# Reordering TensorE's and ScalarE's steps in the second attention pass of a graph network, and pairing the small operations of its dense pass

## The chip, the cores and the metric

One Trainium2 chip; the kernel runs on one of its cores. The metric is the device time of one execution in microseconds (us), lower is better. TensorE does matmuls and transposes, VectorE and ScalarE element-wise work, GpSimd element-wise work and indirect transfers (gathers and scatters of rows), and SyncE (SP) only issues direct transfers. All five run their own queues in order and meet at semaphores.

## The reference

Four layers over a graph of N = 50,000 nodes with 256 features and E = 12,500 edges, each with residual and layer norm:

```python
x = _layernorm(x + gin(x, src, dst, edge_weight))      # sums over edges, two dense layers with batch norm
x = _layernorm(x + gat(x, edge_index, W, a))           # attention over edges, rows without an edge give 0
x = _layernorm(x + attention(x, edge_attr_8, Wq, Wk, Wv, Wo, src, dst))
x = _layernorm(x + self_loop_gat(x, edge_index, W, att_src, att_dst, bias))   # every node has a loop
# of the third:
attn = einsum('ehd,ehd->eh', k[src], q[dst]) + attn_bias
a = exp(attn - segment_max(attn, dst)[dst]);  a = a / segment_sum(a, dst)[dst]
out = segment_sum(v[src] * a[:, :, None], dst).reshape(n, F) @ Wo.T
```

A node that no edge reaches keeps what the layers make of its own row alone: three layer norms in a row, and in the last layer `elu(x3 @ W + bias)`. There are only 12,500 edges for 50,000 nodes, so most nodes are of this kind.

## The kernel before

The program is a chain of phases with a barrier between two of them. First the edges are sorted and the first layer's sums are made; `mlp` computes its dense layers, feature-major, into `Y2`. Then come the two passes that the change touches, with the edge pass of the second layer (`gat_edges`) and the scores of the third between them.

**The dense pass, `nodes` (L1121 to L1355).** It computes for every node what it would be without edges, and stores the rows after layers one and two (`X1`, `X2`) and the final one (`out`). The work is cut in 100 chunks of 500 nodes (one load and one store of each tensor), and each chunk in two tiles of 250 nodes (125 partitions, J = 2 rows each). Per tile: ScalarE `relu` (batch norm and relu of `Y2` into `z`); TensorE `turn_z`; VectorE `add` (u = z + x), `stats`, `aggregate`, `variances1` (three small operations that give the variances of three layer norms in a row); ScalarE `rsqrt1` (Ln and Exp); VectorE `means` (one operation on six elements); GpSimd `first_two` (x1 and x2, two operations each) and ScalarE `third` (x3); TensorE `turn_x3`, ScalarE `copy_x3`, TensorE `product`, ScalarE `exps`, VectorE `elus`, GpSimd `add` (v = elu + x3, one operation of 512 elements); VectorE `stats2`, `aggregate2`, `variances2`; ScalarE `rsqrt2`; VectorE `outs` (two operations).

Each engine's order is written out by hand as a list of (lag, step); `run_stages` goes through it once per iteration, and a step with lag k handles tile t - k in iteration t:

```python
PE    [(8, product), (6, turn_x3), (1, turn_z)]
ACT   [(12, rsqrt2), (9, exps), (7, copy_x3), (5, third), (3, rsqrt1), (0, relu)]
DVE   [(13, outs), (2, add), (11, stats2), (9, elus), (2, stats1), (11, aggregate2), (4, means), (2, aggregate1), (11, variances2), (2, variances1)]
POOL  [(10, add), (5, first_two)]
SP    [(8, store_out), (4, store), (0, load)]      # in chunks
```

**The second attention pass, `attention_sums` (L1928 to L2106).** It goes over 100 columns of 125 edges, sorted by destination, and a last one for sums that cross partitions: 101 iterations, tile 'at' below. VectorE makes weighted rows (`messages`), the running segment sum (`add`), `keep_lead`, `denominators`, `reciprocals` and `quotients`, which writes the normalised row sum `on` (L2092). TensorE turns `on` (`turn`, L1998), ScalarE copies it to `onT` (`copy`, L2040), TensorE multiplies by Wo (`product`, L2006), VectorE adds the node's row (`residual`, L2101: u) and takes its moments, ScalarE normalises it to x3 (`norm`), TensorE turns it (`turn_x3`, L2014, one PSUM buffer), ScalarE copies it (`copy_x3`, L2051), TensorE multiplies by the last layer's weights (`product_x3`, L2022 to L2024), and ScalarE takes that out of PSUM (`keep_xp`: L2056, and L2057 for `ends`). SP loads and stores rows, GpSimd scatters them. The orders:

```python
PE    [(0, carry_over), (7, product_x3), (5, turn_x3), (2, product), (1, turn)]
ACT   [(8, keep_xp), (5, copy_x3), (4, norm), (0, copy)]
DVE   [(0, messages), (3, residual), (0, add), (4, stats), (0, keep_lead), (0, denominators), (4, aggregate), (1, quotients), (0, reciprocals), (4, last)]
```

`product_x3` for tile t waits for `keep_xp` of tile t - 2 (two PSUM buffers), and `turn_x3` of tile t for `copy_x3` of tile t - 1.

## Time and profile before

| | |
|---|---|
| median of 3 runs | 4757.65 us (4750.59 to 4759.39) |
| the profiled execution | 4765.5 us, of which the span of its instructions is 4763.8 us |
| dense pass | 1766 to 2761 us |
| edge pass of layer two (not changed) | from about 2765 to 3420 us |
| second attention pass | 3774 to about 4206 us |

Times in the profile are counted from the start of the span. PE is TensorE's matmuls, PEld its weight loads, DVE VectorE, ACT ScalarE, POOL GpSimd. A line of the timeline merges equal instructions of one engine that follow each other; its brackets give the engine's idle time before and who ended it. The last instruction of the engine before may end a little after the next starts, since they are pipelined.

### The profile page before, as it was taken

What the parts mean: (1) busy time and instruction counts of PE and PEld (TensorE: products, weight loads), DVE (VectorE), ACT (ScalarE), POOL (GpSimd) and SP (SyncE); (2) the same over time, 40 slices, a digit from 0 to 9 for tenths busy, and PEclk for the clock granted to TensorE, in tenths of its full rate; (3) what the DMA queues carried; (4) which work ended last, traced back from release to release, by engine and by line L of the source; (5) the groups of instructions that cost most, each with busy time, mean ns of one, the idle gap of its engine ahead of it and who ended that gap; (6) DMA issues with size and microseconds to landing.
All of it is one profiled execution on the core that took longest, in us unless ns stands there. A gap on an engine that the chain in (4) does not pass through costs nothing. (4 is left out here: it accounts for less than half of the span.)

```text
span 4763.8 us, 90855 instructions
## 1 busy us (share of the span) xinstructions
PE 3204.6 (67%) x16514; PEld 2413.6 (51%) x16514; DVE 3460.4 (73%) x12339; ACT 2663.8 (56%) x6336; POOL 3034.6 (64%) x2926
## 2 busy tenths in 40 slices
PE   4999934447999988777777767777699577720000
PEld 2799812226888865555555545555588444410000
DVE  7788733335555559999999988888755666611998
ACT  0688712224666558878887758878644255510444
POOL 0466668883443337777777768888778355565888
PEclk9999955558999989999999977777699799965555
DMA  1788723333444448888888733333355266642343
GB/s 41 193 237 237 207 71 80 79 79 116 159 162 163 158 159 268 261 263 260 261 261 262 245 93 99 98 98 99 99 128 128 77 180 178 179 111 70 110 110 93
DMA packets 450180, 734.76 MB, mean 154 GB/s; under 512 B 171319, under 2 KB 284845, under 8 KB 450028
## 3 DMA queue, kind: packets, MB, share of 16 engines
q1 hardware_dynamic: 276204, 571.18, 39.8%
q0 software_dynamic: 173824, 162.17, 14.1%
q14 instruction: 131, 1.07, 0.1%
q8 instruction: 21, 0.34, 0.0%
HBM read 351.68 MB, written 389.16 MB: 156 GB/s over the span
## 5 line engine op out<-in xcount | busy, mean ns | idle before, releaser
L1209 PE MATMUL nodes_xp<-w_self,nodes_x3T 128*125 128x256 f32 x1600 | 448.4, 403 | 232.3 <-DVE nodes_elu L1315 232.3
L1081 POOL TENSOR_TENSOR mlp_r_parts<-mlp_r,mlp_r_parts 128x500 fp32r<-128x500 f32 x200 | 253.5, 1267 | 405.0 <-ACT mlp_r_parts L1067 395.7
L1345 POOL TENSOR_SCALAR nodes_x<-nodes_u,nodes_r,nodes_nm 125x256 f32<-125x256 f32 x800 | 448.3, 574 | 79.1 <-DVE nodes_nm L1308 79.1
L1209 PEld LDWEIGHTS nodes_xp<-w_self,nodes_x3T 128*125 128x125 f32 x1600 | 268.4, 187 | 312.3 <-issue 196.1
L1353 POOL TENSOR_TENSOR nodes_v<-nodes_elu,nodes_x 125x512 f32<-125x512 f32 x200 | 253.7, 1269 | 221.9 <-DVE nodes_elu L1315 220.8
L775 PE MATMUL gram<-gin_both,gin_am 125*128 125x257 f32 x404 | 206.1, 665 | 267.7 <-DVE gin_both L758 255.4
L1106 DVE BATCH_NORM_STATS2 mlp_stats<-mlp_y 128x500 f32 (+1 forms) x200 | 136.2, 681 | 256.9 <-ACT mlp_y L1057 256.9
L178 POOL DMA_INDIRECT by_src<-rank_recs,rank_place x100 | 119.7, 1197 | 289.9 <-DVE rank_recs L504 289.3
L775 PEld LDWEIGHTS gram<-gin_both,gin_am 125*128 125x128 f32 x404 | 118.1, 322 | 355.7 <-issue 324.2
L1020 PE MATMUL mlp_y<-mlp_hT,mlp_w 128*128 128x500 f32 x1200 | 297.0, 396 | 1.9 <-DVE mlp_hT L1100 1.2
L1020 PE MATMUL mlp_y<-mlp_r_parts,mlp_w 128*128 128x500 f32 x1200 | 287.3, 388 | 0.8 <-ACT mlp_y L1057 0.8
L564 PE MATMUL gram<-rank_xc 125*128 125x257 f32 (+1 forms) x1600 | 279.1, 328 | 0.0
L564 PEld LDWEIGHTS gram<-rank_xc 125*128 125x128 f32 x1600 | 249.2, 191 | 22.4
L728 DVE SCALAR_TENSOR_TENSOR gin_acc<-gin_acc,same,gin_msg 125x256 f32<-125x256 f32 x100 | 48.4, 484 | 287.4 <-ACT gin_msg L700 207.0
L1065 ACT ACTIVATE mlp_r<-mlp_y,affine 128x500 f32<-128x500 f32 x200 | 154.0, 770 | 182.7 <-PE mlp_y L1020 182.7
L178 POOL DMA_INDIRECT out<-att_fin,write x101 | 124.8, 1236 | 200.5 <-DMA att_fin<-G 193.8
L1020 PEld LDWEIGHTS mlp_y<-mlp_r_parts,mlp_w 128*128 128x128 f32 x1200 | 225.2, 188 | 47.4 <-POOL mlp_r_parts L1081 1.1
L1222 ACT ACTIVATE nodes_z<-nodes_y,affine 128x250 f32<-128x250 f32 x400 | 216.2, 588 | 50.7 <-ACT nodes_r L785 39.1
L1020 PEld LDWEIGHTS mlp_y<-mlp_hT,mlp_w 128*128 128x128 f32 x1200 | 218.0, 188 | 41.6 <-DVE mlp_hT L1100 1.4
L1816 PE MATMUL self_cps<-self_acc,carry 125*125 125x260 f32 x2 | 1.2, 716 | 352.4 <-DVE self_acc L1801 352.4
L700 ACT ACTIVATE gin_msg<-gin_xd,srec 125x256 f32<-125x256 f32 x100 | 50.7, 507 | 308.0 <-DMA gin_xd<-x,other 308.0
L1241 ACT ACTIVATE nodes_x<-nodes_u,nodes_nm,nodes_r 125x256 f32<-125x256 f32 x400 | 219.1, 601 | 0.0
(397 smaller groups left out, 11588.9 us busy)
## 6 DMA issues: line engine op xcount, KB each, us to landing
X<-nodes_x SPq DMA_DIRECT2D x200, 448.0 KB
Y<-mlp_y SPq DMA_DIRECT2D x100, 500.0 KB
nodes_y<-Y SPq DMA_DIRECT2D x100, 500.0 KB
rank_xin<-x SPq DMA_DIRECT2D x100, 448.0 KB
XP<-rank_xc SPq DMA_DIRECT2D x100, 448.0 KB
mlp_h<-XP SPq DMA_DIRECT2D x100, 448.0 KB
nodes_x<-x SPq DMA_DIRECT2D x100, 448.0 KB
out<-nodes_out SPq DMA_DIRECT2D x100, 448.0 KB
```

Of the source, the lines that this page charges most:

```text
L178: self.pool.indirect_dma_start(table, bass.IndirectOffsetOnAxis(index, 0), rows, None, bounds_check=self.bound, oob_is_err=False).then_inc ...
L564: mm = pe.matmul(gram[:, m, 128 * m:F + 1], xc[:, s, j, 128 * m:128 * m + 128], xc[:, s, j, 128 * m:F + 1], start=False, stop=True, skip_g ...
L775: mm = pe.matmul(gram[:, m, 0:F + 1], am[:, s, 128 * m:128 * m + 128], both[:, s, 0:F + 1], start=False, stop=True, skip_group_check=True)
L1020: mm = pe.matmul(out[:, m, 0:CH], w[:, a, k, 128 * m:128 * m + 128], rows[:, s, b, k, :], start=((k, a, b) == terms[0]), stop=((k, a, b) = ...
L1065: act.activation(r[:, s, m, :], y1[:, m, 0:CH], ACT.Relu, bias=aff[:, 1, m:m + 1], scale=aff[:, 0, m:m + 1]).then_inc(s_r, 1)
L1081: pool.tensor_tensor(rp[:, s, 1, m, :], r[:, s, m, :], rp[:, s, 0, m, :], ALU.subtract).then_inc(s_rp, 1)
L1106: dve.bn_stats(stats[:, m, at.col, :].rearrange("p o n -> p (o n)"), y[:, s, m, :]).then_inc(s_st, 1)
L1209: pe.matmul(xp[:, b, j, :], x3T[:, s, k, P * j:P * j + P], w_self[:, k, 0:F], start=(k == 0), stop=False)
L1222: act.activation(z[:, s, m, :], y[:, c, m, HC * h:HC * h + HC], ACT.Relu, bias=aff[:, 3, m:m + 1], scale=aff[:, 2, m:m + 1]).then_inc(s_z, 1)
L1241: act.activation(x3[:, at.slot(LONG), j, :], u[:, s, j, :], ACT.Identity, bias=nm[:, s, 2, j:j + 1], scale=r[:, s, 2, j:j + 1]).then_inc(s ...
L1345: pool.tensor_scalar(dst[:, s, j, :], u[:, s, j, :], r[:, s, k, j:j + 1], nm[:, s, k, j:j + 1], ALU.mult, ALU.add).then_inc(done, 1)
L1353: pool.tensor_tensor(v[:, s, :, :], el[:, s, :, :], x3[:, at.slot(LONG), :, :], ALU.add).then_inc(s_v, 1)
```

## The change

In `attention_sums` two lists change, TensorE's and ScalarE's; nothing of VectorE's, SP's or GpSimd's. TensorE's turn of `on` goes from last to first in an iteration, and `turn_x3` and `product_x3` get one lag more; on ScalarE, `copy` goes from last to first, and `keep_xp` from first to third, behind `copy_x3`.

In `nodes`, the small operations are done once for two tiles (in the iterations in which the step's tile is odd, `pairs_only`): `variances1`, `variances2`, `rsqrt1`, `rsqrt2` on twice as many elements, and `means` as three operations instead of one. `u` and `mv` get eight buffers instead of four. The chunks' load buffers `y` and `x` go from two to four, SP's loop from two to four chunks per turn, and its stores from lags 4 and 8 to 7 and 11. Every step after `means` gets one lag more, on all engines.

```diff
-    y, z = ph.sb("y", [128, 2, KH, CH]), ph.sb("z", [128, RING, KH, HC])
-    x, u = ph.sb("x", [P, RING, J, F]), ph.sb("u", [P, RING, J, F])
+    AHEAD = 4
+    y, z = ph.sb("y", [128, AHEAD, KH, CH]), ph.sb("z", [128, RING, KH, HC])
+    x, u = ph.sb("x", [P, 2 * AHEAD, J, F]), ph.sb("u", [P, LONG, J, F])
...
+    def both(at):
+        return slice(at.slot(RING) - 1, at.slot(RING) + 1)
+
+    def pairs_only(step):
+        return lambda at: step(at) if at.slot(PAIR) == 1 else None
...
-                wait(sp, s_z, at.count(4, 4 - 8))
+                c = at.slot(AHEAD)
+                wait(sp, s_z, at.count(4, 4 - 4 * AHEAD))
...
-                wait(sp, s_u, at.count(2, 2 - 4))
+                wait(sp, s_u, at.count(2, 2 - 2 * AHEAD))
...
-            run_stages(sp, [(8, store_out), (4, store), (0, load)], NCH, NCH, unroll=2)
+            run_stages(sp, [(11, store_out), (7, store), (0, load)], NCH, NCH, unroll=AHEAD)
...
-            run_stages(pe, [(8, product), (6, turn_x3), (1, turn_z)], tiles, tiles, LONG, LONG)
+            run_stages(pe, [(9, product), (7, turn_x3), (1, turn_z)], tiles, tiles, LONG, LONG)
...
+            @pairs_only
             def rsqrt1(at):
-                s = at.slot(RING)
-                act.wait_ge(s_q, at.count(3, 3))
+                p = both(at)
+                act.wait_ge(s_q, at.uses(PAIR, 3, 3))
...
-                rsqrt(act, ch, r[:, s, :, :], lnq[:, s, :, :], q[:, s, :, :])
+                rsqrt(act, ch, r[:, p, :, :], lnq[:, p, :, :], q[:, p, :, :])
...
-            run_stages(act, [(12, rsqrt2), (9, exps), (7, copy_x3), (5, third), (3, rsqrt1), (0, relu)], tiles, tiles, LONG, LONG)
+            run_stages(act, [(13, rsqrt2), (10, exps), (8, copy_x3), (6, third), (3, rsqrt1), (0, relu)], tiles, tiles, LONG, LONG)
...
+            @pairs_only
             def variances1(at):
...
-                    dve.tensor_scalar(q[:, s, k, :], mv[:, s, :, 1], m, a, ALU.mult, ALU.add).then_inc(s_q, 1)
+                    dve.tensor_scalar(q[:, p, k, :], mv[:, both_long(at), :, 1], m, a, ALU.mult, ALU.add).then_inc(s_q, 1)
...
+            @pairs_only
             def means(at):
...
-                dve.scalar_tensor_tensor(out=nm[:, s, :, :], in0=r[:, s, :, :], scalar=-1.0,
-                                         in1=mv[:, s, :, 0].unsqueeze(1).broadcast_to([P, 3, J]), op0=ALU.mult, op1=ALU.mult).then_inc(s_nm, 1)
+                for k in range(3):
+                    dve.scalar_tensor_tensor(out=nm[:, p, k, :], in0=r[:, p, k, :], scalar=-1.0,
+                                             in1=mv[:, both_long(at), :, 0], op0=ALU.mult, op1=ALU.mult).then_inc(s_nm, 1)
...
-                dve.tensor_scalar(q2[:, s, :], mv2[:, s, :, 1], EPS, None, ALU.add).then_inc(s_q2, 1)
+                dve.tensor_scalar(q2[:, p, :], mv2[:, p, :, 1], EPS, None, ALU.add).then_inc(s_q2, 1)
...
-            run_stages(dve, [(13, outs), (2, add), (11, stats2), (9, elus), (2, stats1), (11, aggregate2), (4, means), (2, aggregate1),
-                             (11, variances2), (2, variances1)], tiles, tiles, LONG, LONG)
+            run_stages(dve, [(14, outs), (2, add), (12, stats2), (10, elus), (2, stats1), (12, aggregate2), (4, means), (2, aggregate1),
+                             (12, variances2), (2, variances1)], tiles, tiles, LONG, LONG)
...
-            run_stages(pool, [(10, add), (5, first_two)], tiles, tiles, LONG, LONG)
+            run_stages(pool, [(11, add), (6, first_two)], tiles, tiles, LONG, LONG)
...
-            run_stages(pe, [(0, carry_over), (7, product_x3), (5, turn_x3), (2, product), (1, turn)], T + 1, unroll=LONG, behind=LONG)
+            run_stages(pe, [(0, carry_over), (1, turn), (8, product_x3), (6, turn_x3), (2, product)], T + 1, unroll=LONG, behind=LONG)
...
-            run_stages(act, [(8, keep_xp), (5, copy_x3), (4, norm), (0, copy)], T + 1, unroll=LONG, behind=LONG)
+            run_stages(act, [(0, copy), (6, copy_x3), (8, keep_xp), (4, norm)], T + 1, unroll=LONG, behind=LONG)
```

## Rows read from the trace of the kernel before

**Rows 1.** Stretches: length, busy us of PE, PEld, DVE, ACT, POOL, clock, DMA share, GB/s.

```profile
1797.40:1808.00 10.60, 10.23 (x53) 6.99 (x51) 10.35 (x41) 9.77 (x26) 9.46 (x14) 1.00 0.94 280
1860.00:2700.00 840.00, 629.95 (x3087) 426.25 (x3086) 833.32 (x2912) 674.14 (x1714) 602.02 (x858) 1.00 0.86 261
2824.00:3383.00 559.00, 424.86 (x1680) 303.67 (x1681) 501.86 (x2313) 451.68 (x1335) 451.76 (x352) 0.77 0.38 99
3860.00:4195.00 335.00, 255.11 (x1054) 155.73 (x1055) 215.72 (x953) 178.44 (x653) 197.32 (x163) 0.96 0.65 179
```

**Rows 2.** All waits of VectorE, 1860 to 2700: us, times, longest.

```profile
DVE nodes_out L1329 <- ACTq L1262: 6.7, 21, 0.3
```

**Rows 3.** Timeline of VectorE, one dense tile: start, us, line, tiles, count.

```profile
2300.48 1.08 DVE L1329 TENSOR_SCALAR nodes_out<-nodes_v,nodes_mv,nodes_r 125x256 f32<-125x256 f32 x2
2301.48 0.67 DVE L1274 TENSOR_TENSOR nodes_u<-nodes_zp,nodes_x 125x512 f32<-125x512 f32 x1
...
2303.32 0.74 DVE L1282 BATCH_NORM_STATS2 nodes_stats<-nodes_u 125x6 f32<-125x256 f32 x2
2303.99 0.22 DVE L1292 BATCH_NORM_AGGREGATE nodes_mv<-nodes_stats 125x2 f32<-125x6 f32 x2
2304.14 0.80 DVE L1308 SCALAR_TENSOR_TENSOR nodes_nm<-nodes_r,nodes_mv 125x6 f32<-125x6 f32 x1
2304.85 0.23 DVE L1292 BATCH_NORM_AGGREGATE nodes_mv<-nodes_stats 125x2 f32<-125x6 f32 x2
2305.01 0.13 DVE L1322 TENSOR_SCALAR nodes_q<-nodes_mv 125x2 f32<-125x2 f32 x1
2305.12 0.32 DVE L1300 TENSOR_SCALAR nodes_q<-nodes_mv 125x2 f32<-125x2 f32 x3
2305.36 0.52 DVE L1329 TENSOR_SCALAR nodes_out<-nodes_v,nodes_mv,nodes_r 125x256 f32<-125x256 f32 x1
```

**Rows 4.** Timeline of GpSimd in the same tile.

```profile
2300.29 2.23 POOL L1345 TENSOR_SCALAR nodes_x<-nodes_u,nodes_r,nodes_nm 125x256 f32<-125x256 f32 x4 [0.26 <-DVE nodes_nm L1308]
2303.64 1.27 POOL L1353 TENSOR_TENSOR nodes_v<-nodes_elu,nodes_x 125x512 f32<-125x512 f32 x1 [1.12 <-DVE nodes_elu L1315]
```

**Rows 5.** Timeline of VectorE in the dense pass's last tiles.

```profile
2740.65 1.32 DVE L1322 TENSOR_SCALAR nodes_q<-nodes_mv 125x2 f32<-125x2 f32 x1
2741.88 0.72 DVE L1329 TENSOR_SCALAR nodes_out<-nodes_v,nodes_mv,nodes_r 125x256 f32<-125x256 f32 x2
2742.53 0.74 DVE L1282 BATCH_NORM_STATS2 nodes_stats<-nodes_v 125x6 f32<-125x256 f32 x2
```

**Rows 6.** Timeline of GpSimd in those.

```profile
2740.68 1.27 POOL L1353 TENSOR_TENSOR nodes_v<-nodes_elu,nodes_x 125x512 f32<-125x512 f32 x1
```

**Rows 7.** Timeline of TensorE, second attention pass, at 2.4 GHz.

```profile
4016.00 0.68 PE L2022 MATMUL att_xp<-w_self,att_x3T 128*125 128x264 f32 x2 [0.97 <-ACT ends L2057]
...
4017.47 0.43 PE L2014 MATMUL att_tp<-ident,att_x_xp 125*128 125x125 f32 x2
4017.74 1.03 PE L2006 MATMUL att_op<-w_o,att_onT 128*125 128x256 f32 x4
4018.61 0.38 PE L1998 MATMUL att_tp<-ident,att_on 125*128 125x125 f32 x2
4019.88 0.46 PE L2022 MATMUL att_xp<-w_self,att_x3T 128*125 128x264 f32 x1 [0.90 <-ACT ends L2057]
```

**Rows 8.** Timeline of VectorE there.

```profile
4018.81 0.42 DVE L2101 TENSOR_TENSOR att_u<-att_op,att_xd 125x256 f32<-125x256 f32 x1 [1.29 <-PE att_op L2006]
...
4020.49 0.39 DVE L2092 TENSOR_TENSOR att_on<-att_acc,att_rr 125x256 f32<-125x256 f32 x1
```

**Rows 9.** Timeline of TensorE, same loop, at 1.2 GHz.

```profile
4100.74 1.21 PE L2022 MATMUL att_xp<-w_self,att_x3T 128*125 128x264 f32 x2 [0.90 <-ACT ends L2057]
...
4105.45 0.63 PE L1998 MATMUL att_tp<-ident,att_on 125*128 125x125 f32 x2
```

**Rows 10.** Timeline of all engines at the first tile of the pass.

```profile
3780.36 0.42 DVE L2092 TENSOR_TENSOR att_on<-att_acc,att_rr 125x256 f32<-125x256 f32 x1
...
3780.84 0.29 PEld L1998 LDWEIGHTS att_tp<-ident,att_on 125*128 125x128 f32 x2 [27.91 <-DVE att_on L2092]
```

**Rows 11.** All instructions of line L2101: ns min, median, max; first and last start.

```profile
L2101 DVE TENSOR_TENSOR att_u<-att_op,att_xd x101: 416/425/426, 3784.1 to 4195.1; 125x256 f32<-125x256 f32 x101
```

More of the change, by code:

```diff
@@ L1135, in nodes, with both_long @@
     el, v, out = ph.sb("elu", [P, RING, J, F]), ph.sb("v", [P, RING, J, F]), ph.sb("out", [P, RING, J, F])
-    st, mv = ph.sb("stats", [P, RING, J, 6]), ph.sb("mv", [P, RING, J, 2])
-    q, lnq, r, nm = (ph.sb(n, [P, RING, 3, J]) for n in ("q", "lnq", "r", "nm"))
+    st, mv = ph.sb("stats", [P, RING, J, 6]), ph.sb("mv", [P, LONG, J, 2])
+    q, lnq, r = (ph.sb(n, [P, RING, 3, J]) for n in ("q", "lnq", "r"))
+    nm = ph.sb("nm", [P, RING, 3, J])
+    PAIR = 2
+    def both_long(at):
+        return slice(at.slot(LONG) - 1, at.slot(LONG) + 1)
+    def both(at):
+        return slice(at.slot(RING) - 1, at.slot(RING) + 1)
+    def pairs_only(step):
+        return lambda at: step(at) if at.slot(PAIR) == 1 else None
     st2, mv2 = ph.sb("stats2", [P, RING, J, 6]), ph.sb("mv2", [P, RING, J, 2])
@@ L1140, in nodes @@
     zp, tp, xp = ph.ps("zp", [P, 2, J, F]), ph.ps("tp", [128, 2, KH, 256]), ph.ps("xp", [P, 2, J, F])
-    s_y, s_x, o_1, o_2, o_o = (ph.pair(n) for n in ("y_loaded", "x_loaded", "x1_stored", "x2_stored", "out_stored"))
+    s_y, s_x = ([ph.sem(f"{n}{k}") for k in range(AHEAD)] for n in ("y_loaded", "x_loaded"))
+    o_1, o_2, o_o = (ph.pair(n) for n in ("x1_stored", "x2_stored", "out_stored"))
     (s_z, s_zp, s_u, s_q, s_r, s_nm, s_x1, s_x2, s_x3, s_t3, s_c3, s_xp, s_ex, s_el, s_v, s_q2, s_r2, s_out) = (
@@ L1267, in add, with stats_of @@
             def add(at):
-                s, c, b = at.slot(RING), at.slot(RING) // 2, at.slot(2)
+                l, c, b = at.slot(2 * AHEAD), at.slot(2 * AHEAD) // 2, at.slot(2)
                 dve.wait_ge(s_zp, at.count(1, 1))
-                dve.wait_ge(s_x[c], at.uses(RING, 32, 32))
-                wait(dve, s_x1, at.count(J, J - J * RING))
-                wait(dve, s_x2, at.count(J, J - J * RING))
-                wait(dve, s_x3, at.count(J, J - J * RING))
-                dve.tensor_tensor(u[:, s, :, :], zp[:, b, :, :], x[:, s, :, :], ALU.add).then_inc(s_u, 1)
-            def stats_of(rows, s_rows, st, s_st, s_mv):
+                dve.wait_ge(s_x[c], at.uses(2 * AHEAD, 32, 32))
+                wait(dve, s_x1, at.count(J, J - J * LONG))
+                wait(dve, s_x2, at.count(J, J - J * LONG))
+                wait(dve, s_x3, at.count(J, J - J * LONG))
+                dve.tensor_tensor(u[:, at.slot(LONG), :, :], zp[:, b, :, :], x[:, l, :, :], ALU.add).then_inc(s_u, 1)
+            def stats_of(rows, ring, s_rows, st, s_st, s_mv):
                 def stats(at):
@@ L1281, in stats, with moments_of @@
                     for j in range(J):
-                        dve.bn_stats(st[:, s, j, :], rows[:, s, j, :]).then_inc(s_st, 1)
+                        dve.bn_stats(st[:, s, j, :], rows[:, at.slot(ring), j, :]).then_inc(s_st, 1)
                 return stats
-            def moments_of(st, s_st, mv, s_mv, s_used, per=1):
+            def moments_of(st, s_st, mv, ring, s_mv, free):
                 def aggregate(at):
                     s = at.slot(RING)
-                    wait(dve, s_used, at.count(per, per - per * RING))
+                    free(at)
                     dve.wait_ge(s_st, at.count(J, J))
```

53 lines of the change are left out of this document (30 added, 23 removed).

## The prediction

> **What bounds the kernel now.** I read the table of stretches first. The change touches two of them. The dense pass (stretch 1860 to 2700) has VectorE busy 99% of the time, with DMA at 0.86 and TensorE always at 2.4 GHz. In the second attention pass (3860 to 4195) nothing is near full: TensorE 76%, VectorE 64%, ScalarE 53%, DMA 0.65, mean clock 0.96 [rows 1]. So the dense pass is VectorE's own time, the attention pass a loop of waits, and each has to be read from its own order of instructions.
>
> Dense: VectorE waited only 6.7 us there, for 21 outputs [rows 2]. But its busy time holds waits inside instructions. One tile takes 4.88 us (outs at 2300.48, again at 2305.36) [rows 3]. The six-element `means` takes 0.80 us, 2304.14 to 2304.94, and GpSimd's add runs 2303.64 to 2304.91 [rows 3, 4]: the small instruction ends when the GpSimd one ends. The two outs take 1.08 us under GpSimd's four row operations, and 0.72 us with GpSimd idle [rows 3 to 5]. The same is seen in the drain: a two-element `variances2` takes 1.32 us, to 2741.97, under an add that ends at 2741.95 [rows 5, 6]. So about 0.7 us of each tile is `means` waiting for GpSimd's add.
>
> Attention: TensorE works from 4016.00 to 4018.99 (2.99 us), then idles 0.90 us until ScalarE has written `ends`; the period is 3.88 us [rows 7]. The loop is turn (last on TensorE), copy of `onT`, `keep_xp` (its first lag on ScalarE), `product_x3` (first on TensorE). VectorE is not in it: its residual starts at 4018.81, just when the product ends, and `on` is ready at 4020.88, where the turn of the next iteration comes about 1.6 us later [rows 7, 8]. Over the whole pass 101 residuals run from 3784.1 to 4195.1, 4.11 us each [rows 11]; the excess over 3.88 is the few stretches at 1.2 GHz.
>
> **Attention part.** The lags and order of VectorE stay. In iteration d it does residual(d-3), then the running sum, stats, lead, denominators, aggregate, and then quotients(d-1), which makes `on`. Product(d-3) is the last TensorE work of iteration d-1; turn(d-1) becomes the first of iteration d. So turn(d-1) needs `on`(d-1), which stands on VectorE's queue behind residual(d-3), which needs the product just issued before that turn. Before, `product_x3`, `turn_x3` and product stood between the two and covered VectorE. Now the cover is gone, and TensorE's queue has nothing it may do meanwhile: `product_x3`, `turn_x3` and product are all behind the waiting turn. The period becomes, at 2.4 GHz:
> TensorE's chain 2.99 [rows 7]; product to residual 0.04 (4018.77 to 4018.81) [rows 7, 8]; residual to end of `on` 2.07 (4018.81 to 4020.88) [rows 8]; `on` to turn 0.06 (3780.78 to 3780.84), and the turn's weight load, now behind a wait instead of behind a matmul, 0.14 (two in 0.29) [rows 10]. Sum 5.30 us.
> The old 0.90 us wait for `ends` goes away, since `keep_xp` is now needed an iteration later; ScalarE's new order (copy, `copy_x3`, `keep_xp`, norm) costs nothing: `copy_x3` must end before `turn_x3`, which comes 1.5 us after the turns (4016.00 to 4017.47 of `product_x3` lies between), and the two copies take 0.8 us. That cover gone would cost under 0.5 us. SP's and GpSimd's queues keep their lags; the deeper `product_x3` (7 to 8) adds one short iteration at the end, some 3 us.
>
> The clock then. TensorE would stand idle for 2.2 of each 5.30 us, where it stood for 0.9 of 3.88. Between 2824 and 3383, in the edge pass before attention, the row shows a mean granted clock of 0.77, so 46% of the time at 1.2 GHz, against 0.96 here [rows 1]. No row shows this loop with longer gaps, so its clock is bounded by 1.00 and 0.50, and I take 0.77, from the nearest pass in which TensorE's work is interrupted. At 1.2 GHz the chain takes 5.34 us (4100.74 to 4106.08) [rows 9], so the period is 5.34 + 0.04 + 2.07 + 0.20 = 7.65. With 46% of the time there, the rate is 0.54/5.30 + 0.46/7.65 = 0.162 tiles per us, 6.17 us per tile. Cost: (6.17 - 4.11) x 100 + 3 = +209 us. Bounds: always 2.4 GHz (5.30 - 4.11) x 100 + 3 = +122; always 1.2 GHz (7.65 - 4.11) x 100 + 3 = +357.
>
> **Dense part.** `means`, `variances1`, `variances2` and both rsqrts run once per two tiles. Take the start of stats1 as zero (2303.32). GpSimd's add runs 0.32 to 1.59; then stats2, elus and the rest follow as in the rows. In the iteration of the pair, `means` is three instructions instead of one: the first still ends with the add, the other two cost 0.08 each, the step of `variances1` (three in 0.24) [rows 3]. Nothing else changes: 4.88 + 0.15 = 5.03 us. In the other iteration VectorE reaches the outs at 0.67 + 0.15 + 0.16 = 0.98. The add still holds to 1.59. If the outs wait for it as for the row operations, the first ends at 1.73 (0.14 after the lock is free: the pair that ends at 2301.56 follows GpSimd's second operation, which ends near 2300.29 + 2 x 0.56 = 2301.41, by 0.15). GpSimd's next operation, pushed back by that 0.14, ends at 1.59 + 0.14 + 0.56 = 2.29, the second out at 2.44, and u's add starts 0.08 before; from there to the next stats1 it is 1.84 (2301.48 to 2303.32) [rows 3, 4]. Sum 4.20 us. Mean of the two 4.61, a gain of 0.27 per tile; over the 187 tiles of the steady part -50 us.
> If the outs didn't wait, they would end their two steps of 0.33 at 1.63, and the iteration would take 3.47, the mean 4.25. No row has these outs under that add; the row operations and the two-element operation are the nearest [rows 3 to 6], and I take that they wait. The Trainium skill (SBUF — State Buffer, section "Who interferes with whom") says that a VectorE instruction in a 2-port mode, which tensor_scalar between SBUF tiles can enter, and a GpSimd instruction exclude each other for a whole instruction; by this rule the outs wait and the part gives -50, without it it would be stopped by DMA, at about -112.
> DMA: a tile moves 261 GB/s x 4.88 = 1.28 MB. At 280 GB/s and 0.94 busy (1797 to 1808) that is 4.56 us, and at share 1.00 it is 4.28 [rows 1], so DMA lies just below 4.61 and caps the part at (4.88 - 4.28) x 187 = -112. Four load buffers send loads two chunks earlier. On SP's queue stores move from lag 4 and 8 to 7 and 11, against loads whose slots free two chunks later and rows that come one tile later; store and load stand in the same order in time, so I cost the move at nothing. Covered are the loads, which no VectorE row waited for [rows 2]; were a load to be late, VectorE's `add` and then everything waits. The ScalarE saving (two small pairs of activations per two tiles) is off the path, ScalarE being 80% busy [rows 1]. All lags after `means` grow by one: one drain iteration more, +3 us, against a quicker fill; I take both as zero. Lower bound of the gain: none, if the stalls come back in the odd iteration in full.
>
> **Sum.** The profiled execution took 4765.5 us (span 4763.8, 1.7 around it), 8 above the median of 4757.65. 4765.5 + 209 - 50 = 4924.5; on the median of the runs, 4917 us.
>
> **Rivals.** (1) TensorE's clock stays full in attention: 4757.65 + 122 - 50 = 4830. For it: the pass keeps 0.96 now. Against: the edge pass's 0.77 [rows 1]. Chance 0.17. (2) Mostly 1.2 GHz: 4757.65 + 357 - 50 = 5065; chance 0.10. (3) The dense gain ends at DMA's floor: 4757.65 + 209 - 112 = 4855; chance 0.06. (4) The dense pass gains nothing, as stores, loads and the add's lock take it back: 4967; chance 0.05. (5) Faster: the exposed VectorE segment is not exposed, because `on` comes before the product ends, and only the 0.90 wait goes: 3.00 per tile, (3.00 - 4.11) x 100 = -111, with the dense -50 in all 4597. It needs the segment from residual to `on` hidden; against it stands VectorE's order. The point where the whole change breaks even is an attention period of 4.11 + 0.50 = 4.61, an exposed segment of 2.07 - 0.69 = 1.38 us. Chance 0.05, with all cases faster. (6) Nothing moves in either part: 0.02.
> My forecast has 0.55. The range reaches from a full clock to one that is low for most of the time (80%: 7.03 per tile, +295): 4810 to 5030. A difference within 0.2% can't be told from no change here. Faster 0.05, same 0.02, slower 0.93.
>
> **What would show it.** Attention: the wait of TensorE for `ends` gone, and in its place TensorE waiting for `on` about 2.3 us per tile, VectorE's residual still waiting for the product, residuals spaced 5.3 us at 2.4 GHz and 7.6 at 1.2, mean clock near 0.77. Dense: tiles alternating near 5.0 and 4.2 us, the long `means` only once per pair, outs drawn out under GpSimd's add, DMA at 0.9 and 276 GB/s. A TensorE wait for `on` under 1.4 us, or dense tiles still at 4.88, would make me wrong.

## The result, and the profile after

The changed kernel takes 4965.5 us (median of 4 runs, 4960.8 to 4973.6), against 4755.3 us of the kernel before in the same session (4750.6 to 4759.4): a ratio of 1.0443, with a 95% interval of 1.0431 to 1.0456. It is slower by 210 us. The forecast was 4917 us, with a range of 4810 to 5030.

The first view to open is the table of stretches. Of the kernel after, in the steady part of the dense pass and over the whole second attention pass (from its first residual to its last); the columns are those of [rows 1]:

```profile
1860.00:2650.00 790.00, 669.45 (x3022) 453.28 (x3022) 761.38 (x2604) 583.23 (x1345) 597.67 (x841) 0.91 0.86 272
3741.50:4394.70 653.20, 434.37 (x1271) 264.12 (x1271) 264.23 (x1178) 213.47 (x779) 229.90 (x191) 0.68 0.40 109
```

The same whole pass in the kernel before:

```profile
3784.10:4195.10 411.00, 312.13 (x1279) 191.27 (x1278) 266.59 (x1179) 215.33 (x783) 233.69 (x193) 0.95 0.63 174
```

In the dense pass DMA moves 272 GB/s where it moved 261, and VectorE is still busy 96% of the time. TensorE's clock has a mean of 0.91 there, where it was 1.00; VectorE's list of waits further down has no wait for TensorE, so the rows show no cost of it. In the attention pass VectorE, ScalarE and GpSimd are busy as long as before, but TensorE is busy 434 us instead of 312 with the same work, for its clock has a mean of 0.68: 64% of the time at 1.2 GHz. By phase, from the first to the last instruction on its tiles, the two profiled executions give: dense pass 990.7 us before, 954.4 after (-36.3); edge pass of layer two 654.6 and 648.4 (-6.2); third layer (scores, maxima and the pass that was changed) 781.3 and 1025.6 (+244.3); last layer 540.6 and 540.3. So the loss is all in one place, and the dense part gives back a seventh of it.

All instructions of the residual's line after the change; before, the same line stands in [rows 11]:

```profile
L2128 DVE TENSOR_TENSOR att_u<-att_op,att_xd x101: 423/425/426, 3741.5 to 4394.7; 125x256 f32<-125x256 f32 x101
```

The instruction costs what it did, 425 ns; 100 steps take 653.2 us instead of 411.0, 6.53 us each instead of 4.11. The view of waits says why. TensorE's longest wait over the pass, before:

```profile
PE att_xp L2022 <- ACT ends L2057: 88.5, 94, 1.1
```

All its waits, after:

```profile
PE att_tp L2025 <- DVE att_on L2119: 218.0, 99, 2.5
PE att_tp L2041 <- ACT att_x3T L2078: 0.8, 1, 0.8
```

VectorE's longest wait over the pass, first before, then after:

```profile
DVE att_u L2101 <- PE att_op L2006: 141.8, 100, 3.3
```

```profile
DVE att_u L2128 <- PE att_op L2033: 388.3, 101, 5.2
```

The wait of TensorE for `ends`, 0.90 us per tile in [rows 7], is gone. In its place the turn waits for `on` in 99 tiles of 101. VectorE waited for the product before too, but for 141.8 us in all and now for 388.3: each stands still while the other works. The timeline shows one round. TensorE after:

```profile
4019.43 0.43 PE L2025 MATMUL att_tp<-ident,att_on 125*128 125x125 f32 x2 [2.16 <-DVE att_on L2119]
4019.70 0.61 PE L2049 MATMUL att_xp<-w_self,att_x3T 128*125 128x264 f32 x2
4020.24 0.32 PE L2050 MATMUL att_xp<-bias,one 3*125 3x256 bf16 x1
4020.49 1.13 PE L2051 MATMUL att_xp<-w_self,att_x3T 128*125 128x264 f32 x2
4021.41 0.62 PE L2041 MATMUL att_tp<-ident,att_x_xp 125*128 125x125 f32 x2
4021.83 1.92 PE L2033 MATMUL att_op<-w_o,att_onT 128*125 128x256 f32 x4
4025.90 0.44 PE L2025 MATMUL att_tp<-ident,att_on 125*128 125x125 f32 x2 [2.16 <-DVE att_on L2119]
```

An earlier round, whose work is all at 1.2 GHz:

```profile
3861.32 0.68 PE L2025 MATMUL att_tp<-ident,att_on 125*128 125x125 f32 x2 [2.16 <-DVE att_on L2119]
...
3864.66 1.91 PE L2033 MATMUL att_op<-w_o,att_onT 128*125 128x256 f32 x4
3868.73 0.43 PE L2025 MATMUL att_tp<-ident,att_on 125*128 125x125 f32 x2 [2.16 <-DVE att_on L2119]
```

VectorE in that round:

```profile
3866.61 0.42 DVE L2128 TENSOR_TENSOR att_u<-att_op,att_xd 125x256 f32<-125x256 f32 x1 [4.75 <-PE att_op L2033]
...
3868.29 0.39 DVE L2119 TENSOR_TENSOR att_on<-att_acc,att_rr 125x256 f32<-125x256 f32 x1
3868.60 0.19 DVE L2113 RECIPROCAL att_rr<-att_den 125x8 f32<-125x8 f32 x1
```

From the residual to the end of `on` it is 2.07 us (3866.61 to 3868.68), exactly what [rows 8] gave, and TensorE's idle 2.16 is that segment with the two hand-overs. The clock is to be read off the durations: two equal pairs of `product_x3` matmuls take 0.61 us at 4019.70 and 1.13 at 4020.49. Stretches cut at these places, the first three in the round from 4019.43 and the others in the next:

```profile
4019.43:4020.50 1.07, 1.07 (x6) 0.60 (x6) 0.54 (x5) 0.60 (x3) 0.26 (x1) 1.00 0.00 0
4020.50:4023.70 3.20, 3.20 (x9) 2.01 (x8) 0.00 (x0) 1.59 (x7) 2.13 (x2) 0.52 0.48 117
4023.70:4025.90 2.20, 0.04 (x1) 0.00 (x1) 2.12 (x10) 0.00 (x0) 0.00 (x0) 0.92 0.58 159
4025.90:4026.96 1.06, 1.06 (x5) 0.59 (x5) 0.69 (x5) 0.59 (x3) 0.00 (x0) 1.00 0.08 31
4026.96:4030.10 3.14, 2.90 (x9) 1.85 (x8) 0.01 (x1) 1.60 (x7) 2.34 (x2) 0.58 0.40 108
4030.10:4032.30 2.20, 0.00 (x0) 0.00 (x0) 2.20 (x10) 0.00 (x0) 0.04 (x1) 0.50 0.58 182
```

In the first round TensorE has 2.4 GHz for one microsecond, works on at 1.2 GHz (0.52), and has the full clock again in the gap in which it has nothing to do (0.92), and for the first microsecond of the next burst. In the second round burst and gap are both slow (0.58, 0.50). The whole pass agrees: the granted clock has a mean of 0.82 in TensorE's 99 gaps of over half a microsecond (216.8 us together) and of 0.61 in the rest, in which it works. So a part of the full clock falls into idle time. Rounds differ: a few are at full clock from end to end, as this one, from one turn to the next:

```profile
3902.64:3907.65 5.01, 2.85 (x13) 1.81 (x13) 2.66 (x15) 2.18 (x8) 2.38 (x2) 1.00 0.39 109
```

The dense pass. VectorE after, over two tiles:

```profile
2300.41 1.00 DVE L1349 TENSOR_SCALAR nodes_out<-nodes_v,nodes_mv,nodes_r 125x256 f32<-125x256 f32 x2
2301.34 0.68 DVE L1290 TENSOR_TENSOR nodes_u<-nodes_zp,nodes_x 125x512 f32<-125x512 f32 x1
...
2303.99 0.95 DVE L1327 SCALAR_TENSOR_TENSOR nodes_nm<-nodes_r,nodes_mv 125x4 f32<-125x4 f32 x3
...
2305.89 1.16 DVE L1349 TENSOR_SCALAR nodes_out<-nodes_v,nodes_mv,nodes_r 125x256 f32<-125x256 f32 x2 [0.45 <-ACTq L1278]
2306.97 0.67 DVE L1290 TENSOR_TENSOR nodes_u<-nodes_zp,nodes_x 125x512 f32<-125x512 f32 x1
```

and GpSimd:

```profile
2299.67 1.27 POOL L1380 TENSOR_TENSOR nodes_v<-nodes_elu,nodes_x 125x512 f32<-125x512 f32 x1 [1.65 <-DVE nodes_elu L1334]
2300.92 2.37 POOL L1372 TENSOR_SCALAR nodes_x<-nodes_u,nodes_r,nodes_nm 125x256 f32<-125x256 f32 x4
2303.51 1.26 POOL L1380 TENSOR_TENSOR nodes_v<-nodes_elu,nodes_x 125x512 f32<-125x512 f32 x1 [0.22 <-DVE nodes_elu L1334]
```

The tiles alternate, u's adds being 5.63 us apart (2301.34 to 2306.97) and then 3.82; the long `means` (0.95 us, three instructions, the last of which ends at 2304.94, just behind GpSimd's add at 2304.77) come once per pair. New is the 0.45 us before the outs. It stands in the view of VectorE's waits, 1860 to 2650, where [rows 2] had 6.7 us in 21 waits:

```profile
DVE nodes_out L1349 <- ACTq L1278: 25.5, 64, 0.4
```

### The profile page after: what moved, and what is told of

It is laid out like the page before. It is cut to its first block and busy times, and to the rows that moved or that the text cites. A ratio compares the mean times of both kernels' runs of the same rounds, so it can differ in the third digit from the quotient of the medians.

```text
span 4962.7 us, 89141 instructions
## 1 busy us (share of the span) xinstructions
PE 3365.8 (68%) x16514; PEld 2503.4 (50%) x16514; DVE 3389.2 (68%) x12039; ACT 2567.7 (52%) x5936; POOL 3036.1 (61%) x2926
## 5 line engine op out<-in xcount | busy, mean ns | idle before, releaser
L1223 PE MATMUL nodes_xp<-w_self,nodes_x3T 128*125 128x256 f32 x1600 | 489.3, 432 | 138.3 <-DVE nodes_elu L1334 137.1
L1372 POOL TENSOR_SCALAR nodes_x<-nodes_u,nodes_r,nodes_nm 125x256 f32<-125x256 f32 x800 | 459.7, 589 | 76.6 <-DVE nodes_nm L1327 68.2
L1223 PEld LDWEIGHTS nodes_xp<-w_self,nodes_x3T 128*125 128x125 f32 x1600 | 293.7, 204 | 216.8 <-issue 131.4
L2128 DVE TENSOR_TENSOR att_u<-att_op,att_xd 125x256 f32<-125x256 f32 x101 | 42.9, 424 | 388.3 <-PE att_op L2033 388.3
L2067 ACT COPY att_onT<-att_tp 128x250 f32<-128x250 f32 x101 | 37.2, 368 | 434.6 <-PE att_tp L2025 434.6
L1020 PEld LDWEIGHTS mlp_y<-mlp_hT,mlp_w 128*128 128x128 f32 x1200 | 218.0, 188 | 41.5 <-DVE mlp_hT L1100 1.4
L1349 DVE TENSOR_SCALAR nodes_out<-nodes_v,nodes_mv,nodes_r 125x256 f32<-125x256 f32 x400 | 212.3, 570 | 32.4 <-ACTq L1278 31.0
```

What stands on the lines that cost most here:

```text
L1020: mm = pe.matmul(out[:, m, 0:CH], w[:, a, k, 128 * m:128 * m + 128], rows[:, s, b, k, :], start=((k, a, b) == terms[0]), stop=((k, a, b) = ...
L1223: pe.matmul(xp[:, b, j, :], x3T[:, s, k, P * j:P * j + P], w_self[:, k, 0:F], start=(k == 0), stop=False)
L1349: dve.tensor_scalar(out[:, s, j, :], v[:, s, j, :], mv2[:, s, j, 0:1], r2[:, s, j:j + 1], ALU.subtract, ALU.mult).then_inc(s_out, 1)
L1372: pool.tensor_scalar(dst[:, s, j, :], u[:, at.slot(LONG), j, :], r[:, s, k, j:j + 1], nm[:, s, k, j:j + 1], ALU.mult, ALU.add).then_inc(do ...
```

## The experiments

Each edit is against the changed kernel unless it says otherwise. A ratio is that to the kernel before on the same chip (4757.5, 4749.3, 4749.1 and 4752.4 us in the four sessions), with its 95% interval. "Spacing" is the mean distance of two residuals in the second attention pass.

### The two parts by themselves

`e1_dense_alone`: the attention pass has its old lists again.

```diff
-            run_stages(pe, [(0, carry_over), (1, turn), (8, product_x3), (6, turn_x3), (2, product)], T + 1, unroll=LONG, behind=LONG)
+            run_stages(pe, [(0, carry_over), (7, product_x3), (5, turn_x3), (2, product), (1, turn)], T + 1, unroll=LONG, behind=LONG)
...
-            run_stages(act, [(0, copy), (6, copy_x3), (8, keep_xp), (4, norm)], T + 1, unroll=LONG, behind=LONG)
+            run_stages(act, [(8, keep_xp), (5, copy_x3), (4, norm), (0, copy)], T + 1, unroll=LONG, behind=LONG)
```

> The dense part of the change alone, the attention pass as before. Theory: the two parts add, and the dense pass is worth what its phase lost between the two traces (990.7 to 954.4 us, -36), so about 4757 - 36 = 4720 us. Rival: the time that the dense pass gained is given back in the edge pass that follows, whose clock differs between executions: 4735 to 4757.

4714.3 us, 0.9914 (0.9885 to 0.9943): -43 us; the dense pass has 952.3 us.

`e2_attention_alone`: the kernel before with the two new lists (the same diff the other way round).

> The attention part of the change alone, the dense pass as before. Theory (turn first exposes VectorE's segment): residuals 6.5 us apart instead of 4.1, about 4757 + 244 = 5000 us. Rival (the new dense pass takes part in the slowing): under 4980.

5009.0 us, 1.053 (1.0501 to 1.056): +252 us; spacing 6.52 us, dense pass 990.2. The parts add up: 252 - 43 is 209, and 210 was measured. The two can be studied one by one.

### Which move of the attention part costs the time

`e3_turn_last` puts the turn back to the end, keeps the deeper lags of `turn_x3` and `product_x3`, and gives ScalarE its old order. `e4_scalar_order_old` has ScalarE's list of e3 and leaves the turn first. The two differ in nothing but the turn's place.

```diff
-            run_stages(pe, [(0, carry_over), (1, turn), (8, product_x3), (6, turn_x3), (2, product)], T + 1, unroll=LONG, behind=LONG)
+            run_stages(pe, [(0, carry_over), (8, product_x3), (6, turn_x3), (2, product), (1, turn)], T + 1, unroll=LONG, behind=LONG)     # e3 alone
...
-            run_stages(act, [(0, copy), (6, copy_x3), (8, keep_xp), (4, norm)], T + 1, unroll=LONG, behind=LONG)
+            run_stages(act, [(8, keep_xp), (6, copy_x3), (4, norm), (0, copy)], T + 1, unroll=LONG, behind=LONG)     # e3 and e4
```

> The changed kernel with TensorE's turn of the attention pass put back to the end of the iteration and ScalarE's list in the old order; the deeper lags of turn_x3 and product_x3 stay. Theory: VectorE's segment is covered again, and with one lag more TensorE has no wait for ends either, so TensorE's 3.0 us of work sets the period: residuals 3.0 to 3.4 us apart, 101 of them 310 to 345 us, the kernel 4965 - 330 = about 4635 us (4620 to 4670). Rival (the deeper lags or ScalarE's share are what slowed the pass): over 4800.

> The changed kernel with ScalarE's list in the old order (keep_xp, copy_x3, norm, copy) and the turn still first on TensorE. Theory: ScalarE is not in the loop; same as the changed kernel, residuals 6.5 us apart, 4965 us within 15. Rival (copy and evacuation order on ScalarE is part of the loss): at least 50 us away from it.

e3: 4667.4 us, 0.9811 (0.9784 to 0.9838), spacing 3.54. e4: 4965.4 us, 1.0436 (1.0407 to 1.0465), spacing 6.54. The turn's place alone is worth 298 us, and ScalarE's order nothing. e3 also shows what the deeper lags are worth (`turn_x3`, `copy_x3` and `product_x3` together, which no run separates): the wait for `ends` is in no list of its TensorE's waits, and a tile takes 3.54 us instead of 4.11. It fell short of the 3.0 to 3.4 expected, since a wait of another kind came forward. ScalarE's waits in the attention pass of e3:

```profile
ACT att_x_xp L964 <- DMA XP<-att_x_xp,write: 126.7, 85, 3.7
```

`norm` waits for the buffer that GpSimd's scatter (`put`) is still reading.

`e5_quotients_early` leaves the turn first and makes `on` early instead: VectorE's quotients go ahead of the residual.

```diff
-            run_stages(dve, [(0, sums.messages), (3, residual), (0, add), (4, stats), (0, sums.keep_lead), (0, denominators),
-                             (4, aggregate), (1, quotients), (0, reciprocals), (4, last)], T + 1, unroll=LONG, behind=LONG)
+            run_stages(dve, [(0, sums.messages), (1, quotients), (3, residual), (0, add), (4, stats), (0, sums.keep_lead), (0, denominators),
+                             (4, aggregate), (0, reciprocals), (4, last)], T + 1, unroll=LONG, behind=LONG)
```

> The changed kernel, turn still first on TensorE, but VectorE makes on (quotients) before the residual instead of after the running sum, stats, lead, denominators and aggregate. Theory: the product to on to turn loop is cut, since on no longer stands behind the residual; TensorE's 3.0 us or the scatter's slots set the period: residuals 3.0 to 3.6 us apart, about 4965 - 300 = 4665 us (4640 to 4700). Rival (a turn at the head of TensorE's queue is slow in itself): over 4850.

4676.4 us, 0.9852 (0.9836 to 0.9869), spacing 3.58. TensorE's waits for `on` shrink from 218.0 us to:

```profile
PE att_tp L2025 <- DVE att_on L2119: 8.3, 14, 1.3
```

So a turn in the first place is not slow in itself. Slow is that `on` stood on VectorE's queue behind a residual that needs the product issued just ahead of the turn. This is the point at which the fifth rival (a hidden segment, and a faster kernel) would have come true, and the run shows that its price was right in sign and too large: with the segment hidden the kernel is 1.5% faster than before, with a spacing of 3.58 us where the rival had 3.00.

### How much of it is the clock

`e6_filler` adds twelve bf16 matmuls of 248 columns behind each product; they write a PSUM area that nobody reads and only keep TensorE busy while it would wait. The rest of the loop, the wait for `on` included, is as in the changed kernel; the matmuls lie inside that wait.

```diff
+FILL = 12
...
                 mm.then_inc(s_o, 1)
+                if not at.is_lead:
+                    for _ in range(FILL):
+                        pe.matmul(cps[:, 264:512], env["ident_bf"][:, 0:P], env["zrow"][:, 0:248], start=True, stop=True)
```

> The changed kernel with 12 bf16 matmuls of 248 columns added on TensorE behind each product of the attention pass, on zeros, into columns of a PSUM bank that nothing reads, so inside the wait for on. Theory (of the 2.4 us by which a tile takes longer, some 0.9 is the exposed segment and 1.5 is the clock at 1.2 GHz): granted clock of the pass goes from 0.68 to over 0.9 and residuals from 6.5 to 5.0 to 5.3 us apart, about 4965 - 135 = 4830 us (4810 to 4860). Rival (the clock does not follow the idle time between TensorE's pieces of work, or does not matter): 4965 us or more, as the matmuls only add work.

4815.7 us, 1.0138 (1.0121 to 1.0155). The stretch of its whole pass, and TensorE's timeline for one tile:

```profile
3749.30:4249.90 500.60, 406.58 (x2470) 310.38 (x2469) 267.55 (x1178) 213.08 (x779) 231.79 (x191) 1.00 0.50 142
```

```profile
4003.80 0.43 PE L2028 MATMUL att_tp<-ident,att_on 125*128 125x125 f32 x2 [0.89 <-DVE att_on L2125]
4004.06 0.61 PE L2055 MATMUL att_xp<-w_self,att_x3T 128*125 128x264 f32 x2
...
4005.61 1.03 PE L2036 MATMUL att_op<-w_o,att_onT 128*125 128x256 f32 x4
4006.48 1.43 PE L2040 MATMUL att_cps<-zrow,ident_bf 128*125 128x248 bf16 x12
4008.81 0.43 PE L2028 MATMUL att_tp<-ident,att_on 125*128 125x125 f32 x2 [0.89 <-DVE att_on L2125]
```

With more work for TensorE the kernel is 150 us faster than the changed one. The clock is at 1.00, the spacing is 5.01 us. That splits the loss of 2.42 us per tile (6.53 against 4.11): 0.90 us is the exposed segment at full clock, less the wait for `ends` that went, and 1.52 us the slower clock that the longer gap brings. (The 4.11 holds some slow clock of its own, mean 0.95; against the full-clock 3.88 of [rows 7] the first part is 1.13 us.) The full-clock period of 5.01 us is also that of the changed kernel's round from 3902.64 to 3907.65 above.

### The dense pass

`e7_two_buffers`: two load buffers instead of four, stores at the old lags of 8 and 4 chunks; the pairing stays.

```diff
-    AHEAD = 4
+    AHEAD = 2
...
-            run_stages(sp, [(11, store_out), (7, store), (0, load)], NCH, NCH, unroll=AHEAD)
+            run_stages(sp, [(8, store_out), (4, store), (0, load)], NCH, NCH, unroll=AHEAD)
```

> The changed kernel with two load buffers of the dense pass instead of four, and the stores at chunk lags 4 and 8 as before. Theory: no load was late before and none is now, so tiles stay at 3.8 and 5.6 us; only the two waits at tiles 11 and 12 (6.7 and 9.9 us between adds, stores behind loads of four chunks) go, so 4965 - 10 = about 4955 us. Rival (the paired pass needs the deeper loads): relu waits for y, 4980 us or more.

5068.2 us, 1.0675 (1.0658 to 1.0693), dense pass 1046.8 us against 954.4. ScalarE's waits over its dense pass, first line:

```profile
ACT nodes_z L1236 <- DMA nodes_y<-Y: 262.8, 99, 6.4
```

My expectation was wrong and the rival right. The waits of SP's queue, 2000 to 2600, name what holds the load back. First this run, then the changed kernel, then the kernel before:

```profile
SPq L1180 <- DVE nodes_out L1349: 226.6, 58, 5.6
```

```profile
SPq L1174 <- DVE nodes_u L1290: 137.1, 64, 2.8
SPq L1180 <- POOL nodes_x L1372: 43.0, 58, 1.7
```

```profile
SPq L1166 <- DVE nodes_out L1329: 196.8, 61, 3.5
```

With lag 8 the store of the final rows heads the turn of SP's queue and waits for outs that now come a tile later, and the load of the next chunk can only be issued behind it. The wait itself is not new: the kernel before has 196.8 us of it, longest 3.5, and its loads came in time (11.5 us of waits for `y` in the whole pass). Paired, it is 226.6 us and 5.6 at the longest, and with two buffers the load has no slack left for that. At lag 11 with four buffers SP waits for free load slots (L1174), as a queue that runs ahead should, and ScalarE's wait for `y` is not in its list. Buffers and lags together save 92 us that the pairing would otherwise cost. They were changed together here, so how much each does is open. Buffers and lags without the pairing were not run; that the pass owes its gain to the pairing is read from the tiles, which alternate, and from the kernel before, in which no load of the steady part was late. The start of the pass, which I expected to become 10 us shorter, did not: to the fifteenth of u's adds it is 52.7 us here and 52.2 in the changed kernel.

`e8_second_single`: `variances2` and `rsqrt2` once per tile again.

```diff
-            @pairs_only
             def variances2(at):
-                p = both(at)
+                s = at.slot(RING)
...
-                dve.tensor_scalar(q2[:, p, :], mv2[:, p, :, 1], EPS, None, ALU.add).then_inc(s_q2, 1)
+                dve.tensor_scalar(q2[:, s, :], mv2[:, s, :, 1], EPS, None, ALU.add).then_inc(s_q2, 1)
```

(`rsqrt2`, and the wait of the outs for it, in the same way.)

> The changed kernel with variances2 and rsqrt2 done for each tile again, means, variances1 and rsqrt1 still for pairs. Theory: the outs of the even tile wait for rsqrt2 because pairing took an iteration of slack from it (the 0.45 us and the later place among GpSimd's operations); singly, the pair's iteration goes from 5.6 to 5.1 and the other from 3.8 to 3.9 us, mean 4.5 instead of 4.7, 190 tiles x 0.2 = -40 us: about 4925 us, or 4935 if DMA (then near 280 GB/s) holds it. Rival (the wait only moves to another operation): 4960 to 4985, the more as VectorE and ScalarE have more instructions.

4966.5 us (4947.5 to 4974.8), 1.0464 (1.0447 to 1.0482): not the 4925 expected. The dense pass has 944.0 us instead of 954.4, a quarter of what I expected of it, and in the time of the whole kernel even that can't be seen. The mechanism did show: the long interval of the pair fell from 5.6 us to between 5.0 and 5.2, with no wait for `rsqrt2`. But the short one rose from 3.82 to 4.17, and its row says why; VectorE and GpSimd of this run, same tile:

```profile
2303.22 0.55 DVE L1340 TENSOR_SCALAR nodes_q<-nodes_mv 125x2 f32<-125x2 f32 x1
```

```profile
2302.48 1.27 POOL L1378 TENSOR_TENSOR nodes_v<-nodes_elu,nodes_x 125x512 f32<-125x512 f32 x1 [1.12 <-DVE nodes_elu L1333]
```

The two-element `variances2`, 0.13 us elsewhere, lasts until 2303.77, just after GpSimd's add ends at 2303.75. Once it runs in every tile, it pays for the add in the tile in which `means` does not.

`e9_outs_later` is e3 with VectorE's `add` ahead of its outs, which gives `rsqrt2` 0.6 us more.

```diff
-            run_stages(dve, [(14, outs), (2, add), (12, stats2), (10, elus), (2, stats1), (12, aggregate2), (4, means), (2, aggregate1),
+            run_stages(dve, [(2, add), (14, outs), (12, stats2), (10, elus), (2, stats1), (12, aggregate2), (4, means), (2, aggregate1),
```

> The kernel of e3_turn_last with VectorE's outs of the dense pass behind its add of u instead of ahead of it. Theory: the outs of the even tile then come 0.6 us later and rsqrt2 is ready, so the wait of 0.45 us goes and the pair's iteration falls from 5.6 to 5.1 or 5.2 us, the other stays within 0.1 of 3.8; the dense phase 957 - 40 = 917 us (910 to 935) and the kernel 4667 - 40 = about 4627 us. Rival (GpSimd's row operations, not rsqrt2, set when the outs end): no change within 10 us.

4650.4 us, 0.979 (0.9773 to 0.9806): 17 us under e3, about half of what was expected. e3 was timed on another chip, and by the ratios it is 10 us with intervals that overlap; what shows the gain is the dense pass itself, 939.5 us against e3's 957.6. The wait for `rsqrt2` is gone, the intervals are near 4.0 and 5.3 us. The other half went into the outs, which now lie under GpSimd's row operations in both tiles (1.26 us in the long one).

`e11_means_early` tests the lock by itself, on the kernel before: nothing is paired, `means` is only moved ahead of `elus`, away from GpSimd's add.

```diff
-            run_stages(dve, [(13, outs), (2, add), (11, stats2), (9, elus), (2, stats1), (11, aggregate2), (4, means), (2, aggregate1),
+            run_stages(dve, [(13, outs), (2, add), (11, stats2), (4, means), (9, elus), (2, stats1), (11, aggregate2), (2, aggregate1),
```

> The kernel before with one step moved: VectorE's means ahead of elus, where GpSimd is idle. Theory (a VectorE instruction that needs both SBUF ports waits for the whole GpSimd instruction): means falls from 0.80 to about 0.15 us, and variances2, now the first such instruction under GpSimd's add, grows from 0.13 to 0.5 to 0.7 us; GpSimd starts its row operations sooner, so the outs move too: a tile takes 4.3 to 4.9 us, the kernel 4640 to 4757. Rival (the six-element operation with its broadcast operand is slow in itself): means stays at 0.8 us.

4709.9 us, 0.9917 (0.9894 to 0.994). All instructions of `means` in this run:

```profile
L1308 DVE SCALAR_TENSOR_TENSOR nodes_nm<-nodes_r,nodes_mv x200: 140/143/399, 1773.7 to 2689.5; 125x6 f32<-125x6 f32 x100
```

The kernel before has a median of 790 ns for the same instruction on the same six elements. Of the 0.65 us won, 0.2 stay per tile (4.67 to 4.68 us apart instead of 4.88), for now `variances2` lies under the add and takes 0.56. The dense pass has 947.7 us: this one move is worth 43 us there, and the pairing with all its buffers 36.

### Together

`e10_put_sooner` is e3 with GpSimd's `put` at lag 9 instead of 11, so that the buffer for which `norm` waited comes free sooner.

```diff
-            run_unrolled(pool, [(0, put_final), (11, put)], T + 1, LONG)
+            run_unrolled(pool, [(0, put_final), (9, put)], T + 1, LONG)
```

> The kernel of e3_turn_last with GpSimd's scatter of the attention pass (put) at lag 9 instead of 11. Theory: with TensorE's waits gone, ScalarE's norm waits 127 us in all for slots whose rows a late scatter has not stored yet; two iterations sooner frees them: residuals from 3.5 to 3.1 to 3.3 us apart, the kernel 4667 - 30 = about 4637 us (4620 to 4650). Rival (the loads and scatters themselves are at their rate): no change within 10 us.

4650.1 us, 0.9786 (0.9769 to 0.9802), again a ratio whose interval overlaps that of e3; the spacing shows the gain, 3.33 instead of 3.54, or 21 us in 100 tiles. `norm` still waits for the scatter, 104.6 us in 80 tiles where it was 126.7 in 85. The lag was a part of it, a little over half of the 30 us that I expected; what holds the rest of that wait was not followed further.

`e12_combined` is e3 with both of these and `means` ahead of `elus` in the paired kernel.

```diff
-            run_stages(dve, [(14, outs), (2, add), (12, stats2), (10, elus), (2, stats1), (12, aggregate2), (4, means), (2, aggregate1),
+            run_stages(dve, [(2, add), (14, outs), (12, stats2), (4, means), (10, elus), (2, stats1), (12, aggregate2), (2, aggregate1),
```

> All that gained so far in one kernel: the changed kernel with the turn of on last again on TensorE and ScalarE's old order, GpSimd's put with two lags less, VectorE's add ahead of the outs in the dense pass, and the three means of a pair ahead of elus, so that they don't stand under GpSimd's add. Theory (the parts add): 4667 less 17 (put) less 18 (outs later) is 4632; with means early some 0.6 us per pair less in the steady part, at most 0.6 x 93 = 56, of which I expect under half, since DMA has a share of 0.87 in the outs-later run: 4605 to 4635. Rival: the wait for GpSimd's add only moves to the variances of the pair, or DMA holds the dense pass: no gain over 4632, adds mean still 4.5 us apart, dense pass near 940 us.

4609.6 us (4607.8 to 4612.5), 0.9701 (0.9685 to 0.9717): 3.0% under the kernel before and 7.2% under the changed one. It is 58 us under e3. By phase, the dense pass gives 41 of them (957.6 to 916.8 us): 18 are what e9 had, and 23 come with `means`, the only difference between the dense passes of e9 (939.5) and of this run. The third layer gives 14 (729.7 to 715.9), where e10 alone had 18. The dense pass has DMA at 286 GB/s and a share of 0.90, where the prediction's floor for it went by a stretch with 280 at 0.94 [rows 1]:

```profile
1860.00:2600.00 740.00, 606.82 (x2970) 410.54 (x2970) 727.11 (x2558) 571.88 (x1320) 579.13 (x825) 1.00 0.90 286
```

## Why the prediction was right, and where its terms were off

**Direction and mechanism of the attention part: shown.** The wait for `ends` went, the turn waits for `on`, and the whole pass is a relay of TensorE and VectorE; e3 against e4 puts 298 us on the turn's place and nothing on ScalarE's, and e5 takes the loss away by making `on` early and leaves the turn first. The segment of 2.07 us is right to the hundredth.

**Its size, +209 us, was 35 us too small** (+244 in the profiled phase, +252 alone in e2). The term that was mis-sized most is the clock, and a second error, in the opposite direction, hid a part of it. The period at full clock was put at 5.30 us and is 5.01 (e6): TensorE's part from the turn's start to the residual is 2.88 us (4003.80 to 4006.68 in e6), where I had added 2.99, 0.04 and 0.14. The 2.99 had been read over a burst that began behind a wait, so the 0.14 for a start behind a wait was most likely counted twice; no run takes the rest of that difference apart. At 1.2 GHz 7.65 was expected; one round of the changed kernel, from the turn at 3861.32 to that at 3868.73, takes 7.41, its product at the 1.2 GHz duration (1.91 for four where e6 has 1.03); a round with a mean clock of 0.50, from 3826.55 to 3833.97, takes the same. The clock was put at 0.77, from a neighbouring pass, and is 0.68: 64% of the time at 1.2 GHz instead of 46%. By the prediction's formula its own periods with the right clock would have given 6.60 us per tile and +252 us, and the right periods with its clock 5.89 us and +181: that +209 came out no further off is in part luck. The formula has a fault too. With the measured periods and 0.36 of the time at full clock it gives 0.36/5.01 + 0.64/7.41 = 0.158 tiles per us, 6.32 us per tile, and 6.53 were measured: it counts all full clock as work done, and here some lies in the gap. Where TensorE works, the clock is 0.61, so 23% of that time is at 2.4 GHz. The work of a tile is 5.01 - 2.16 = 2.85 us at 2.4 GHz and 7.41 - 2.16 = 5.25 at 1.2; 0.23/2.85 + 0.77/5.25 = 0.227 makes it 4.40 us, and with the mean gap of 2.19 us a tile takes 6.59. The first rival, a clock that stays full, had been given 4830 us; e6 makes it a measurement, 4816.

**The dense part, -50 us, came out at -36 in its phase and -43 in the run by itself** (-27 to -55 by the interval; the dense phase of that run is 38 us shorter). Over the 180 tiles from the fifteenth of u's adds to the 195th, 1822.3 to 2703.3 before and 1820.3 to 2664.5 after, a tile takes 4.69 us instead of 4.89: a gain of 0.20 where 0.27 was forecast. Both intervals were mis-sized, and the errors largely cancel, which is luck. The long one was to be 5.03 and is 5.6. The step that failed is "Nothing else changes": pairing takes a step's slack from the even tile. Before, `variances2`, `rsqrt2` and outs of a tile came in iterations t + 11, t + 12 and t + 13. Paired, the even tile's `variances2` comes at the end of t + 13, and `rsqrt2` and the outs both in t + 14, each the first step of its engine. VectorE then waits 0.45 us for ScalarE, as e9 shows by removing it. The short one was to be 4.20 and is 3.82. That the outs wait for GpSimd's add was right: the add ends at 2300.94 and the first of the outs at 2301.09. Wrong was that GpSimd's next operation would come between the two. The second one followed at once, until 2301.41, and it was GpSimd that waited: its four operations take 2.37 us instead of the 2.23 of [rows 4].

The rule of the Trainium skill on which a rival for the outs was weighed (SBUF — State Buffer, section "Who interferes with whom": a VectorE instruction in a 2-port mode and one of GpSimd exclude each other for a whole instruction) agrees with `variances2` in e8 and e11 (0.55 and 0.56 us under the add instead of 0.13) and with the outs of the changed kernel. `means` is an operation on two input tensors, so this sentence does not speak of it; that it waits too is what e11 shows. The page also says that the one that issues first gets the ports. Here two instructions of VectorE in a row got through ahead of one of GpSimd whose record starts at 2300.92, 0.09 us before that of the second; when each was issued, no row here tells.

**Costed at nothing.** ScalarE's new order: right, e4. SP's stores and loads: right as a sum, not as a reason. "Store and load stand in the same order in time" says nothing of the store that heads the queue and now waits longer; the move was free because of the four buffers and the deeper lags, and e7 prices their absence at 92 us. Fill and drain of the dense pass, taken as zero: right as a sum. Around the eleventh tile u's adds are 6.7 and 9.9 us apart, and GpSimd, 1766 to 1860, shows this for it:

```profile
POOL nodes_x L1372 <- DMA X<-nodes_x: 8.4, 2, 8.2
```

The first of these stores is issued no later than before (1781.94 and 1782.48), but behind the loads of seven chunks instead of four; that these loads hold it up is argued, not tested. The tiles before it come quicker in return: from the start of the pass to the fifteenth add it is 52.3 us before and 52.2 after, from the 195th add to the end 57.4 and 58.0. The whole -36 us is in the steady part.

The floor that DMA was to set, 4.28 us per tile, was too high: at a share of 1.00 the 280 GB/s at 0.94 give 298 GB/s, and the 286 at 0.90 of e12 give 318, by the same reckoning an estimate of 4.0 us. The changed kernel, with 4.69 us, is above either.

## What to carry to other kernels

When engines run hand-written orders in lockstep, draw the ring before moving a step: for each wait, what stands ahead of the awaited instruction on the other engine's queue, and whether that needs something issued just before the waiting one here. A step placed right behind the one that its input waits for turns two engines into a relay, and on TensorE the gap cost again as clock here (0.90 us exposed, 1.52 us of clock per tile), so look for the cheap remedy first: the turn last, or `on` earlier. When steps are paired to save small instructions, count the iterations left for the tile that waits for its partner, on every engine and on the load queue; and before pairing a small instruction, see whether it is long because it stands under another engine's instruction: then moving it can win as much as halving it (43 us in the dense pass of e11, 36 for the pairing).
